# A gated cross-attention kernel whose f32 projections become 16-bit halves, with part of its vector work moved to GpSimd

## The reference

```python
def _layernorm(x, eps=1e-05):
    return (x - mean(x)) / jnp.sqrt(var(x) + eps)          # over the last axis

def xattn(x, context, Wq, Wk, Wv, Wo):                     # 16 heads of 16
    q, k, v = (x @ Wq), (context @ Wk), (context @ Wv)     # split into heads
    scores = einsum('bhid,bhjd->bhij', q, k) * 16 ** -0.5
    attn = softmax(where(mask, scores, -max), axis=-1)
    return einsum('bhij,bhjd->bhid', attn, v) @ Wo         # heads joined

def ffn(x, W1, b1, W2, b2):                                # 256 -> 1024 -> 256
    h = gelu(x @ ternary(W1).T + b1)
    return h @ ternary(W2).T + b2

x = x + tanh(g_xattn) * xattn(_layernorm(x), ctx, Wq, Wk, Wv, Wo)
x = x + tanh(g_ffn) * ffn(_layernorm(x), W1, b1, W2, b2)
```

## Time and profile before

| | us |
|---|---|
| median of three runs | 1668.31 (1665.9 to 1672.3) |
| the profiled execution, its time | 1668.12 |
| the profiled execution, its span | 1666.3 |
| PE busy | 1511.3 (91%) |
| DVE busy | 1487.7 (89%) |
| ACT busy | 938.2 (56%) |
| POOL busy | 668.6 (40%) |
| granted TensorE clock, mean | 0.980 |

### The profile page before, as it was taken

One profiled execution on the slowest core, in us unless ns is written; L12 is line 12 of the kernel. 1 busy time (PEld: TensorE's weight loads), 2 busy tenths in 40 slices (PEclk: granted clock), 3 DMA queues, 4 the chain that ended last, 5 costly groups with the idle time before them and its releaser, 6 DMA issues.

```text
span 1666.3 us, 48258 instructions
## 1 busy us (share of the span) xinstructions
PE 1511.3 (91%) x14501; PEld 1010.6 (61%) x14501; DVE 1487.7 (89%) x4375; ACT 938.2 (56%) x1799; POOL 668.6 (40%) x813
## 2 busy tenths in 40 slices
PE   3899999999999999999999999997999999999998
PEld 2566666666666666666666666664666666666665
DVE  7799999999999999999999999987888888888886
ACT  2465656565656666566656565644555554555554
POOL 5355555455554545554555555452111111111111
PEclk9799999999999999999999999986999999999999
DMA  2333333333333333333333333311010110101101
GB/s 79 89 97 85 94 85 86 97 86 97 83 96 83 97 84 93 87 89 92 86 97 83 98 81 97 80 47 55 27 38 25 38 36 27 38 25 38 38 25 51
DMA packets 207471, 117.93 MB, mean 71 GB/s; under 512 B 24912, under 2 KB 207184, under 8 KB 207440
## 3 DMA queue, kind: packets, MB, share of 16 engines
q1 hardware_dynamic: 207440, 117.54, 26.1%
HBM read 32.53 MB, written 16.78 MB: 30 GB/s over the span
## 4 chain that ended last, share of the span: by engine, by line
PE 54%; DVE 26%; issue 13%; ACT 4%; DVEq 2%; DMA 0%; ACTq 0%
PE bank L1060 12%; PE bank L308 9%; PE bank L1090 5%; PE bank L1089 5%; DVE smax L745 5%; PE bank L332 4%; PE bank L315 4%; PE bank L299 4%; DVE xres L790 3%; DVE rstd L685 3%; DVE k L715 2%; DVE rstd L687 2%; PE bank L387 2%; DVE y L1047 2%; DVE rstd L678 2%
## 5 line engine op out<-in xcount | busy, mean ns | idle before, releaser
L915 POOL TENSOR_TENSOR probl<-prob 128x512 f16<-128x512 f32 x512 | 528.9, 1041 | 535.8 <-ACT prob L597 534.9
L597 ACT ACTIVATE prob<-bank,masks 128x512 f32<-128x512 f32 x512 | 345.2, 687 | 144.9 <-PE bank L367 144.9
L745 DVE TENSOR_REDUCE smax<-bank 128x4 f32<-128x512 f32 x512 | 348.1, 681 | 14.5 <-PE bank L332 10.6
L1076 DVE TENSOR_TENSOR hidl<-hid 128x512 f16<-128x512 f32 x256 | 226.9, 886 | 79.5 <-ACT hid L1071 78.8
L1071 ACT ACTIVATE hid<-bank,b_sb 128x512 f32<-128x512 f32 x256 | 175.9, 687 | 212.3 <-PE bank L1060 206.1
L1060 PE MATMUL bank<-y,w1T 128*128 128x512 f16 x1024 | 262.9, 379 | 29.9 <-DVE y L1047 28.4
L1154 POOL TENSOR_TENSOR xres<-xres,b2g 128x1024 f32 (+1 forms) x32 | 75.7, 2365 | 431.3 <-ACT yln L1024 413.4
L1089 PE MATMUL bank<-w2T,hid 128*128 128x256 f16 x1024 | 237.4, 273 | 1.4 <-ACT w2T L1004 1.4
L1090 PE MATMUL bank<-w2T,hidl 128*128 128x256 f16 x1024 | 237.3, 273 | 0.0
L332 PE MATMUL bank<-k_rows,q_rows 34*128 34x128 f16 x2048 | 228.0, 222 | 6.8 <-DMA q_rows<-smaxT 3.4
L367 PE MATMUL bank<-q_rows,k_rows 50*128 50x128 f16 x2048 | 204.4, 221 | 0.9 <-DMA q_rows<-smaxT 0.9
(11 more groups left out here) (90 smaller groups left out, 2555.7 us busy)
## 6 DMA issues: line engine op xcount, KB each, us to landing
q_rows<-q SPq DMA_DIRECT2D x512, 64.0 KB, 2.6
k_rows<-k SPq DMA_DIRECT2D x512, 64.0 KB, 2.5
xres<-in_x_dram SPq DMA_DIRECT2D x64, 256.0 KB, 2.7
out_dram<-ystage SPq DMA_DIRECT2D x32, 512.0 KB, 2.9
ctx_sb<-in_ctx_dram SPq DMA_DIRECT2D x64, 192.0 KB, 3.1
q_rows<-smaxT SPq DMA_DIRECT2D x128, 8.0 KB
w_raw<-in_L_ffn_W_dram SPq DMA_DIRECT2D x2, 1024.0 KB, 6.7
prob<-in_L_xattn_Wq_dram SPq DMA_DIRECT2D x1, 256.0 KB, 3.9
```

The lines of the kernel that those rows point to most:

```text
L597: act.activation(prob[u][:], st_bank[u % 2][:], ACT.Exp, bias=0.0, scale=masks[g.parity][:, 2 + b:3 + b]).then_inc(exp_done, 1)
L745: dve.tensor_reduce(smax[:, b, u * UH:(u + 1) * UH], sm_bank[u % 2][:].rearrange("p (h j) -> p h j", h=UH), AX.X, ALU.max).then_inc(max_ta ...
L915: pool.tensor_tensor(probl[u][:], prob[u][:], prob[u][:].bitcast(BF16)[:, 1::2], ALU.subtract).then_inc(prob_split, 1)
```

## The change

It does these things, all but the last two in the attention part:

1. **f16 projections.** Weights are held as two f16 halves scaled by 64 (`wq16`, `wk16`, `wv16`, `wo16`). Each f32 product becomes three 16-bit matmuls (high x high, high x low, low x high), so q, k and v take 12 matmuls each for a group, and the output projection 6 for each batch.
2. **Halves in place on POOL.** `xln`, `ctx_sb` and `prob` are f32 tiles. POOL overwrites the lower 16 bits of each element with the f16 rest: `low_x` (128x512), `low_ctx` (128x384), `low_prob` (128x512, as before but into `prob` itself; `probl` is gone). PE now transposes the halves as 16-bit data, 8 instructions instead of 4 for x and for the context, and ACT copies out 1024 f16 elements for each instead of 512 f32. The context is cut 96 + 96 rows instead of 128 + 64.
3. **Norm by four batches.** DVE takes the statistics of four batches once for two groups, in the even one, and makes the seed of the root (`seed_x`). The three Newton steps, 14 small instructions (`root_x`), run on POOL in the even group, two behind each `low_prob` from (0,1) on. x is loaded four batches at a time.
4. **Output halves.** `copy_attnT` writes f16, and a new DVE instruction `low_attn` (128x256, from PSUM) makes the low half, two for each group. `project_out` waits for it.
5. **Value sums in PSUM.** The sum of the two halves goes to a free part of the PSUM bank instead of to `attn`, and `normalise` reads it there. `low_q` and `low_k` are one instruction of 512 elements instead of two of 256.
6. **Padding.** The small matmuls read 64 rows instead of 34 and 50, and write 48 columns instead of 33.
7. **Start.** ACT and DVE make the weight halves (12 instructions each) and DVE clears padding (two memsets of 4096 f16 and two of about 1070).
8. In the feed-forward part only the names of the norm's tiles change.

The core of the diff:

```diff
         def transpose_x(pe, g, tr_free):
...
-            pe.wait_ge(ln_done, 2 * (g.n + 1))
-            for k in range(KD):
-                for b in range(2):
-                    last = pe.transpose(tr_bank[:, k * T + b * S:k * T + (b + 1) * S],
-                                        xln[:, b, k * P:(k + 1) * P], ident[:])
+            pe.wait_ge(x_split, g.n + 1)
+            for part in range(2):
+                for k in range(KD):
+                    for b in range(2):
+                        o = ((part * KD + k) * 2 + b) * S
+                        last = pe.transpose(tr_bank[:].bitcast(F16)[:, o:o + S],
+                                            halves(xln[:, b, k * P:(k + 1) * P], part), ident16[:])
...
         def project_q(pe, g, m):
...
-                last = pe.matmul(pj_bank[:, m * T:(m + 1) * T], wq_sb[:, k, m * P:(m + 1) * P],
-                                 xlnT[:, k, :], start=(k == 0), stop=(k == KD - 1))
+                for i, (wp, xp) in enumerate(SPLIT):
+                    last = pe.matmul(by_batch(m), wq16[:, wp, k, m * P:(m + 1) * P],
+                                     typed(xT16[:, xp, k, :], xp).rearrange("p (b s) -> p b s", b=2),
...
         def project_out(pe, n, tr_free):
...
-            pe.wait_ge(attnT_copied, n + 1)
+            pe.wait_ge(attnT_split, n + 1)
...
+        def low_x(pool, g):
+            pool.wait_ge(ln_done, 2 * (g.n + 1))
+            x = xln[:].rearrange("p b d -> p (b d)")
+            pool.tensor_tensor(x.bitcast(F16)[:, 0::2], x, x.bitcast(BF16)[:, 1::2], ALU.subtract).then_inc(x_split, 1)
...
+        def low_attn(dve, n):
+            dve.wait_ge(attnT_high, n + 1)
+            dve.tensor_tensor(attnT16[:, 1].rearrange("p k t -> p (k t)"), tr_bank[:, 0:KD * S],
+                              attnT16[:, 0].rearrange("p k t -> p (k t)"), ALU.subtract).then_inc(attnT_split, 1)
...
         def dve_group(dve, g, left):
...
+                if g.parity == 0 and left >= 4 and i < SEED_PARTS:
+                    seed_x(dve, g.half + 2, i)
...
+            norm(0)
+            if not first:
+                low_attn(dve, g.batch(0) - 2)
             take_max(dve, g, 1, 2)
-            norm(8)
             if not first:
                 add_attention(dve, g.batch(0) - 2)
...
         def pool_group(pool, g, left):
             for b in range(2):
                 for u in range(UNITS):
                     low_prob(pool, g, b, u)
+                    k = b * UNITS + u
+                    if g.parity == 0 and left >= 4 and k >= 1:
+                        for i in range(2 * k - 2, 2 * k):
+                            root_x(pool, g.half + 2, i)
+                    if b == 0 and u == 0 and left >= 3:
+                        low_ctx(pool, g.after(3))
                     if b == 1 and u == 0 and left >= 1:
                         pick_masks(pool, g.after(1))
+                    if b == 1 and u == 1 and left >= 3:
+                        low_x(pool, g.after(3))
```

More of the change, by code:

```diff
@@ L306, in project_k @@
                 pe.wait_ge(ctxT_copied, g.n + 1)
[L307 to L309 removed]
+            for k in range(2):
+                for i, (wp, xp) in enumerate(SPLIT):
+                    last = pe.matmul(by_batch(m), wk16[:, wp, k, m * P:(m + 1) * P],
+                                     typed(ctxT16[g.parity][:, xp, k, :], xp).rearrange("p (b s) -> p b s", b=2),
+                                     start=(k == 0 and i == 0 and m == 0), stop=(k == 1 and i == 2),
+                                     skip_group_check=True)
             if m == KD - 1:
@@ L313, in project_v @@
         def project_v(pe, g, b):
-            for k, rows in enumerate((P, C1)):
-                last = pe.matmul(pj_bank[:, b * D:(b + 1) * D], ctxT[g.parity][0:rows, k, b * S:(b + 1) * S],
-                                 wv_sb[0:rows, k, :], start=(k == 0), stop=(k == 1))
+            for k in range(2):
+                for i, (wp, xp) in enumerate(SPLIT):
+                    last = pe.matmul(pj_bank[:, b * D:(b + 1) * D],
+                                     typed(ctxT16[g.parity][:, xp, k, b * S:(b + 1) * S], xp),
+                                     wv16[:, wp, k, :], start=(k == 0 and i == 0 and b == 0),
+                                     stop=(k == 1 and i == 2), skip_group_check=True)
             if b == 1:
@@ L658, in ln_part @@
         def ln_part(dve, i, rows, step, base, ready):
-            n = len(rows)
-            half, y, t, shift = (rstd[:, k, 0:n] for k in range(4))
+            half, y, t = (rstd[:, k, :] for k in range(3))
             if i > 0:
@@ L688, in ln_part @@
             else:
-                last = dve.scalar_tensor_tensor(y, t, 1.5, y, ALU.add, ALU.mult)
+                last = dve.scalar_tensor_tensor(norm[:, 0, :] if i == LN_PARTS - 2 else y, t, 1.5, y, ALU.add,
+                                                ALU.mult)
             last.then_inc(step, 1)
@@ new lines, in seed_x @@
+        def seed_x(dve, half, i):
+            past = half - 2
+            if i == 0:
+                dve.wait_ge(x_in, 16 * (half + 1))
+                for b in range(QB):
+                    last = dve.bn_stats(stats[:, b, :], row_of(half * QB + b))
+            elif i == 1:
+                if not (isinstance(half, int) and half == 2):
+                    dve.wait_ge(ln_ready, half)
+                dve.wait_ge(seed_step, past * (SEED_PARTS - 1) + 1)
+                dve.tensor_copy(rstd[:, 2, :], stats[:, :, 1])
+                for b in range(QB):
+                    last = dve.bn_aggr(meanvar[:, b, :], stats[:, b, :])
+            elif i == 2:
+                dve.wait_ge(seed_step, past * (SEED_PARTS - 1) + 2)
+                dve.tensor_scalar(newton[:, 2, :], meanvar[:, :, 1], EPS, -0.5, ALU.add, ALU.mult)
+                last = dve.tensor_scalar(newton[:, 0, :], meanvar[:, :, 1], EPS, None, ALU.add)
+            else:
+                dve.wait_ge(seed_step, past * (SEED_PARTS - 1) + 3)
+                dve.tensor_scalar(newton[:, 1, :].bitcast(I32), newton[:, 0, :].bitcast(I32), -0.5, RSQRT_SEED,
+                                  ALU.mult, ALU.add).then_inc(root_seeded, 1)
+                return
+            last.then_inc(seed_step, 1)
@@ L1011, in norm_y @@
             for i in parts:
-                if i == 3 and not (isinstance(g.half, int) and g.n == 0):
-                    dve.wait_ge(y_done, QB * g.n)
-                rows = [row_of(g.n * QB + b) for b in range(QB)] if i == 0 else (None,) * QB
+                if i == LN_PARTS - 2:
+                    if isinstance(g.half, int) and g.n == 0:
+                        dve.wait_ge(ln_done, B)
+                    else:
+                        dve.wait_ge(y_done, QB * g.n)
+                rows = [row_of(g.n * QB + b) for b in range(QB)] if i == 0 else ()
                 ln_part(dve, i, rows, y_step, g.n * (LN_PARTS - 1), y_ready)
```

374 lines of the change are left out of this document (231 added, 143 removed).

## The result

| | before | changed |
|---|---|---|
| median, us | 1668.42 (1665.9 to 1672.3) | 2076.64 (2051.0 to 2086.3) |
| ratio, with its 95% interval | 1 | 1.239 (1.232 to 1.246) |
| profiled execution, its time | 1668.12 | 2073.93 |
| its span | 1666.3 | 2072.2 |

The changed kernel takes 408 us more. The forecast was 2095 us, with a range of 1840 to 2260. The ratio compares fast runs alone and so leaves out the slowest of the changed kernel's four (2086.3 us), whose time is in the median. The four differ by 35 us, which matters for the small differences further down.

What follows compares the result with a forecast made beforehand. DVE was taken to hold the pace, 16.96 us a group. 1668.1 + 183 (longer loop) + 10 (start) - 6 (last groups) = 1855 us; +242 for the low clock made the forecast 2095 us, range 1840 to 2260.

Steps and rivals of the forecast that it cites:

- The loop: Attention part: PE's x transposes wait for POOL's low_x; 18.8 us odd, 21.1 even, mean 3.0 longer than before, +183 us.
- 1, copy of x done: Eight 16-bit transposes of x on PE, then ACT's copy_xT; ends at t = 1.7.
- 3, `low_attn` done: high_v on ACT, low_v and low_attn on DVE; t = 6.5, four bn_stats add 1.35 us in even groups.
- 4, context transposed: PE's output projection, scores (0,1), weigh (1,3), half of q and context transposes; ends at t = 9.0.
- step 5: ACT's copies, halves and exponentials back to back, copy_ctxT to exp (1,0); 5.6 us, t = 14.6.
- step 6: POOL's low_prob (1,0), masks, low_prob (1,1), low_x; 3.9 us, t = 18.5; root pairs add 1.0 us in even groups.
- The clock: PE's gaps in attention halve its clock; +6.6 us for a group wholly at low clock, +403 us; +242 us taken.
- The factor 0.6: Share of the time in attention groups taken to run at the low clock; gives +242 us.
- the 1.7 us counted there: At the low clock, q's second half and k on PE make ACT wait; 1.7 us a group.
- the 0.9 us behind it: At the low clock, project_out ahead of scores (1,1) on PE becomes later than POOL; 0.9 us a group.
- (c): Rival: x transposes find low_x done, DVE's 13.5 us a group is the period; 1460 us; chance 0.05.
- (a): Rival: PE's clock mostly holds, the loop of 19.95 us stays; 1855 to 1970 us; chance 0.21.

Runs made afterwards that it cites:

- e1: The changed kernel with low_x moved on POOL to stand ahead of low_prob (1,0), not behind low_prob (1,1); 1730.7 us, ratio 1.035.
- e2: The changed kernel with low_attn of a group's first batch moved on DVE ahead of the next group's low_v; 1923.8 us, ratio 1.153.
- e6: The changed kernel with the four bn_stats of seed_x moved behind add_attention on DVE; 2029.4 us, ratio 1.216.
- e7: The changed kernel with the root instructions behind low_prob (1,0) and (1,1) moved behind (1,2) and (1,3); 2038.9 us, ratio 1.223.
- e3: The changed kernel with 12 idle matmuls on constants on PE ahead of each wait for low_x; 1933.2 us, ratio 1.158.
- e12_queue: Over e10, the wait for the roots' end and the load of x put behind the first moves on SP's queue; 1552.5 us, ratio 0.932.
- e4: The changed kernel without the padding of the small matmuls (34 and 50 rows, 33 columns); 2091.8 us, ratio 1.253.
- e5: The changed kernel with the edits of e1 and e2 together; 1677.2 us, ratio 1.005.
- e8: The changed kernel with the edits of e1, e2, e6 and e7 together; 1713.8 us, ratio 1.026.
- e9: Over e5, low_ctx on POOL moved behind low_prob of unit (1,2) instead of (0,0); 1711.4 us, ratio 1.026.
- e10: Over e5, the context's load put on SP's queue ahead of the wait for the roots' end and load of x; 1647.9 us, ratio 0.987.

## Why the prediction was right, step by step

**The loop.** It was put at 18.8 us for an odd group and 21.1 for an even one at full clock. The rows of the even group, with t from the end of `low_x` at 699.96:

| step | forecast t, full clock, with the even group's additions | measured t |
|---|---|---|
| 1, copy of x done | 1.7 | 1.7 |
| 3, `low_attn` done | 7.85 | 9.8 |
| 4, context transposed | 10.35 | 14.4 |
| 5, POOL starts `low_prob` (1,0) | 15.95 | 20.27 |
| 6, `low_x` done | 21.1 | 24.98 |

DVE of this group shows step 3, and what stands ahead of `low_attn` (L828):

```profile
707.23 0.88 DVE L875 SCALAR_TENSOR_TENSOR v<-bank,masks,v 128x256 f16<-128x256 f32 x2 [1.80 <-ACT v L620]
708.02 1.40 DVE L768 BATCH_NORM_STATS2 stats<-xres 128x6 f32 x4
709.34 0.41 DVE L828 TENSOR_TENSOR attnT<-bank,attnT 128x256 f16<-128x256 f32 x1
```

POOL shows step 6 (the masks and one of each pair of roots are left out):

```profile
720.23 1.04 POOL L1055 TENSOR_TENSOR prob<-prob 128x512 f16<-128x512 f32 x1
721.23 0.20 POOL L809 TENSOR_TENSOR newton<-newton 128x4 f32<-128x4 f32 x1
...
722.48 1.04 POOL L1055 TENSOR_TENSOR prob<-prob 128x512 f16<-128x512 f32 x1
723.47 0.20 POOL L813 TENSOR_TENSOR newton<-newton 128x4 f32<-128x4 f32 x1
...
723.90 1.04 POOL L819 TENSOR_TENSOR xln<-xln 128x512 f16<-128x512 f32 x1
```

Steps 1, 5 and 6 have the lengths that were summed (4.7 us for step 6 against 4.9 with the roots, 5.9 for step 5 against 5.6). The whole surplus, 3.9 us, is gathered between t = 2 and t = 14, while the granted clock is 0.50. `low_attn`, `low_x` and `low_prob` take 0.41, 1.04 and 1.04 us; their nearest rows had given 0.4 and 1.03. Writing in place costs nothing that can be seen. e1, e2, e6 and e7 each take one part out. e2, e6 and e7 pay as the sum says, and e1 pays 346 us where 357 or more were forecast. That shows the loop and not only the coincidence of its length.

**The clock.** Forecast 0.6 of 6.6 us a group, 4.0 us. Measured 3.9 us in the even group (24.98 against 21.1) and 4.0 in the odd one (22.81 against 18.8). The factor 0.6 was the weakest number of the prediction, a choice between bounds, and that it fits so well is partly luck: the parts were not all right. The clock comes back at about 715, so step 5 runs at full speed, and the 1.7 us counted there and the 0.9 us behind it don't occur; steps 1 to 4 get their full 4 us, although the transposes of x, 0.4 of it, ran at full clock (0.62 us); where that 0.4 went is open. e3 shows 143 us of the 242 to be the clock's, and its clock is still 0.90, so the whole effect is larger. The sum itself, 1855 + 242, is 2097, and the prediction gives 2095.

**What was mis-sized or not seen.** DVE's own need is 14.0 us a group (414.8 us over 29.6 groups), not 13.5; in e12_queue it is 13.6 (627.0 us over 46.3 groups). A part of it is `round_max` and `low_max` (L892, L899), which were 175 and 176 ns on average and are now 446 and 344: 0.9 us a group in all. The padding was put at 0 and gains 15 us (e4). The start was put at +10 and the last groups at -6; together they come to -3 (406 less 409). The wait of `low_ctx` for its load was not foreseen at all; it cost nothing here and was the next limit as soon as the loop was broken. DVE's statistics and seed take 1.2 us a group (1.5 forecast).

**The rivals.** (c), that the chain is hidden and DVE's need of 13.5 us sets the pace, 1460 us, was no matter of durations but of the fixed order: with `low_x`, one `low_attn` and the load of x with its wait in other places, the same work runs at 15.13 us a group, 1552 us, with DVE busy for 90% of the time. The prediction rightly gave it little, since it was asked of the order as it stood. (a), that the clock holds, fell; its lower end, 1855, fits e3's line at a clock of 1.00, which is an estimate.

**The experiments' own misses** were larger than that of the prediction. e5, e8, e9 and e10 were expected at 1490 to 1540 us and came out at 1648 to 1714. In e5, e9 and e10 the error was the same: a wait was taken out of the sum in full, and the next one behind the same cause was not looked for. On SP's queue three things stood behind one wait for the roots: the load of x that needs it, the load of the context, and the moves of q and k. Moving a reader (e9) or one of them (e10) only showed the next. Moving the wait (e12) ended it.

## What to carry to other kernels

When an engine gets a new job on the way from one stage to the next, follow the chain once round the group and place the job in its engine's order right where its input is ready: here one instruction of 1 us in the wrong place cost 346 us. Gaps of 3 to 4 us in TensorE's work cost twice, once as waiting and once as slow matmuls behind them. When a removed wait doesn't pay in full, list everything that is queued behind the thing still waited for, the queue that issues the transfers included, and move the wait rather than its victims.

## What the runs showed of the hardware

**A gap is paid behind it.** The gap of 3.3 us ahead of 700.0 in the changed kernel, and in e5_both the one of 3.2 us ahead of 704.20, left the clock at half for about 13 and 7 us; in e10_load_first one of 2.35 us was followed by some 3 us of it. The low stretches differ by a factor of four, the gaps by one of 1.4. In the changed kernel PE stood still for 2.66 us more within the low stretch; in the other two it had no second gap of that length there. The Trainium skill (TensorE: Matmul & The Clock Gate, "Why this matters for your kernels") warns of gaps between bursts of matmuls; the runs agree with it, and e3 gives the price of the opposite: 12 idle matmuls a group, -143 us.

**Padding, higher clock.** Padding with zeros (64 rows instead of 34 and 50) together with 48 instead of 33 columns left the number and the busy time of the instructions alone, to 1%, and raised the clock from 0.64 to 0.72 (e4_pads_off).

**DVE stands while POOL works.** In e10_load_first, DVE's `low_max` (L899), an instruction on 16 columns, ends when POOL's `low_prob` ends; where POOL is idle it takes 0.17 us:

```profile
713.83 0.96 DVE L899 SCALAR_TENSOR_TENSOR smax<-smax 128x16 f16<-128x16 f32 x1
...
713.73 1.04 POOL L1053 TENSOR_TENSOR prob<-prob 128x512 f16<-128x512 f32 x1
...
732.74 0.17 DVE L899 SCALAR_TENSOR_TENSOR smax<-smax 128x16 f16<-128x16 f32 x1
```

The Trainium skill (SBUF — State Buffer, "Who interferes with whom") says that a DVE instruction with two inputs in SBUF contends with a GpSimd instruction that reads SBUF; `low_max` has two such inputs, and the rows fit.

The prediction said that no row shows this block. Rows of the kernel before do, for an instruction of the norm on two columns. It ends when POOL's `low_prob` ends, and takes 0.15 us where POOL is idle:

```profile
714.95 0.98 DVE L678 TENSOR_SCALAR rstd<-rstd 128x2 int32<-128x2 int32 x1
...
714.87 1.04 POOL L915 TENSOR_TENSOR probl<-prob 128x512 f16<-128x512 f32 x1 [0.86 <-ACT prob L597]
...
731.71 0.15 DVE L678 TENSOR_SCALAR rstd<-rstd 128x2 int32<-128x2 int32 x1
```

So a part of the 4.5 us that the norm's small instructions took on DVE was standing and not work. In the changed kernel `round_max` and `low_max` stand in their place, 0.9 us a group more than before (0.6 us in e12_queue, where they take 264 and 387 ns on average).
